# Splits on GpSimd in pieces of 512 columns, and down products of two experts in the two column halves of TensorE

## The reference

```
xl = x2 @ Wdown.T                       # x2: 1024 tokens x 256, xl: 1024 x 64
p  = top 8 of sigmoid(x2 @ Wg.T) + biases, normalised, times 2.5
for e in range(16):
    ye  = xl @ rw1[e].T * _sqrelu(xl @ rwg[e].T) @ rw2[e].T    # 64 -> 128 -> 64
    acc = acc + w_dense[:, e:e + 1] * ye
out = shared + acc @ Wup.T              # shared: the same form on x2, without a router
```

## Time and profile before

| | |
|---|---|
| median of 3 runs | 1700.2 us (1696.12 to 1702.62) |
| the profiled execution | 1699.6 us, its span 1698.3 us |
| TensorE busy | 1468.8 us, 86% |
| VectorE busy | 1240.4 us, 73% |
| ScalarE busy | 1127.9 us, 66% |
| GpSimd busy | 782.1 us, 46% |
| mean granted clock of TensorE | 0.945 |

### The profile page before, as it was taken

How to read it: one execution, slowest core, us unless ns; L and a number is a source line. 1 busy time by engine, 2 the same in 40 slices (tenths; PEclk the granted TensorE clock), 3 DMA queues, 4 the chain that set the end, 5 groups by cost and what they waited for, 6 DMA issues and landing times.

```text
span 1698.3 us, 25299 instructions
## 1 busy us (share of the span) xinstructions
PE 1468.8 (86%) x8373; PEld 713.5 (42%) x8460; DVE 1240.4 (73%) x2184; ACT 1127.9 (66%) x2020; POOL 782.1 (46%) x585
## 2 busy tenths in 40 slices
PE   5688888787878799879798989899889999999979
PEld 3243343343323243324344454444544455455445
DVE  6765766666686356568888858899689997788937
ACT  3567767658655755368677858687478776788724
POOL 3014013014020000058766848787476877577823
PEclk8697997999889999989999999999999999999989
DMA  4001200200331100010000100000000000000000
GB/s 152 1 1 33 48 2 8 53 1 5 56 114 62 51 1 5 20 39 6 1 1 20 39 20 1 6 26 1 5 25 1 26 1 1 1 1 1 1 1 26
DMA packets 20488, 36.69 MB, mean 22 GB/s; under 512 B 4898, under 2 KB 15238, under 8 KB 19334
## 3 DMA queue, kind: packets, MB, share of 16 engines
q1 hardware_dynamic: 20358, 35.07, 7.1%
HBM read 26.53 MB, written 1.15 MB: 16 GB/s over the span
## 4 chain that ended last, share of the span: by engine, by line
PE 37%; issue 7%; DVE 5%; POOL 4%; ACT 4%; POOLq 0%; ACTq 0%; DVEq 0%
PE BK L581 37%; POOL arena L1870 3%; DVE arena L1512 2%; DVE arena L1495 1%; ACT arena L1758 1%; ACT arena L1766 1%; ACT arena L1751 1%; POOL arena L1867 0%; POOL arena L1876 0%; DVE arena L886 0%; POOL arena L1847 0%; ACT L1751 0%; PE BK L866 0%; PE BK L1177 0%; POOL arena L909 0%
## 5 line engine op out<-in xcount | busy, mean ns | idle before, releaser
L581 PE MATMUL BK<-arena 128*128 128x512 bf16 (+9 forms) x8043 | 1420.8, 376 | 184.4 <-DVE arena L1495 34.0
L581 PEld LDWEIGHTS BK<-arena 128*128 128x128 bf16 (+8 forms) x8130 | 675.5, 115 | 898.4 <-issue 245.5
L1870 POOL TENSOR_TENSOR arena<-arena 128x512 f32<-128x512 f32 (+1 forms) x352 | 508.0, 1443 | 178.4 <-ACT arena L1751 154.9
L1512 DVE TENSOR_TENSOR arena<-arena 128x512 bf16<-128x512 f32 (+1 forms) x416 | 517.8, 1253 | 40.0 <-ACT arena L1758 39.6
L1751 ACT ACTIVATE arena<-BK,arena 128x512 f32<-128x512 f32 (+1 forms) x416 | 286.1, 688 | 131.2 <-PE BK L581 117.9
L1327 DVE TENSOR_REDUCE arena<-BK 128x1 f32<-128x512 f32 x384 | 244.2, 683 | 65.4 <-PE BK L581 64.1
L1659 ACT ACTIVATE arena<-BK 128x512 f32<-128x512 f32 (+1 forms) x416 | 226.1, 598 | 76.3 <-PE BK L581 69.6
L1758 ACT CAST arena<-arena 128x512 bf16<-128x512 f32 (+1 forms) x416 | 253.4, 609 | 0.0
L1766 ACT ACTIVATE arena<-BK 128x512 bf16<-128x512 f32 (+1 forms) x256 | 130.2, 508 | 88.0 <-PE BK L581 87.1
L1495 DVE CUSTOM_DVE_ANT_0 arena<-BK,arena 128x512 bf16<-128x512 f32 (+1 forms) x256 | 145.6, 569 | 37.0 <-PE BK L581 33.6
L1800 POOL TENSOR_TENSOR arena<-arena 128x256 f32<-128x256 f32 (+6 forms) x45 | 30.2, 672 | 209.3 <-ACT arena L1598 207.0
(11 more groups left out here) (170 smaller groups left out, 866.7 us busy)
## 6 DMA issues: line engine op xcount, KB each, us to landing
arena<-arena SPq DMA_DIRECT2D x144, 50.0 KB, 2.2
arena<-in_ctxT SPq DMA_DIRECT2D x8, 800.5 KB, 4.5
arena<-in_ctxk SPq DMA_DIRECT2D x4, 768.0 KB
arena<-in_wo SPq DMA_DIRECT2D x1, 2048.0 KB, 7.9
arena<-in_wqT SPq DMA_DIRECT2D x1, 2048.0 KB, 7.6
arena<-in_x SPq DMA_DIRECT2D x4, 256.0 KB, 11.0
arena<-in_rsel SPq DMA_DIRECT2D x1, 1024.0 KB, 9.2
arena<-in_rw1T SPq DMA_DIRECT2D x1, 1024.0 KB, 5.1
```

What stands on the lines that cost most here:

```text
L581: return T.matmul(out_, lhsT, rhs, start=start, stop=stop, skip_group_check=True)
L1512: V.tensor_tensor(Pl[k][0:m, :], P1[k][0:m, :], Ph[k][0:m, :], ALU.subtract).then_inc(p_low, 1)
L1870: G.tensor_tensor(acc[0:m, g % 2, :], acc[0:m, g % 2, :], P1[k][0:m, :], ALU.add).then_inc(summed1, 1)
```

## The change

Three things. GpSimd's splits are cut: the expert weights in eight pairs of a cast and a subtraction of 512 columns, `cy` in three subtractions (448, 448, 449 columns), `vc` in pieces of three tiles (384 columns). The semaphore `rw_split` counts to 8 where it counted to 1.

The down products are issued as a pair, behind every second `up`: that of the even expert into partitions 0 to 63 of bank 6, that of the odd one into 64 to 127, each half summing eight experts. `ac` copies 128 partitions, and the last product (`tl`) takes all 128 rows of `xlX` and `wu_`, which adds the halves. `dn_done` counts pairs.

For this `hh` gets a fourth buffer; the room comes from `rr`, as Relu and Square now both work in `r2`.

```diff
@@ stage1 of the plan
-                piece("dn", p)
+                if p % 2:
+                    piece("dn", p)
@@ buffers
-        rr = sb("rr", [128, 2, 512], F32, F0)
-        hh = sb("hh", [128, 3, 512], F32, F0)
+        hh = sb("hh", [128, 4, 512], F32, F0)
@@ TensorE, "dn"
-                    if p % E == 0:
+                    if p % E == 1:
                         pe.wait_ge(o_copied, 16)
                         pe.wait_ge(ac_done, p // E)
                     pe.wait_ge(*emptied("up", p, 2))
                     pe.wait_ge(ld_moe["rw2"], 16)
-                    mm(BK[6][0:64, :], rw2[:, p % E, :], hh[:, p % 3, :], start=(p % E == 0),
-                       stop=(p % E == E - 1)).then_inc(dn_done, 1)
+                    for q in (p - 1, p):
+                        hr = slice(64 * (q % 2), 64 * (q % 2) + 64)
+                        t = mm(BK[6][hr, :], rw2[:, q % E, :], hh[:, q % 4, :], start=(q % E < 2), stop=(q % E >= E - 2))
+                    t.then_inc(dn_done, 1)
@@ TensorE, "tl"
-                    mm(o, xlX[0:64, 128 * k:128 * k + 128], wu_[0:64, :], start=False).then_inc(full[i], 1)
+                    mm(o, xlX[:, 128 * k:128 * k + 128], wu_[:, :], start=False).then_inc(full[i], 1)
@@ VectorE, "up"
-                    dve.wait_ge(dn_done, s - 2)
-                    V.tensor_tensor(hh[:, s % 3, :], BK[g3][:, :], tt_[:, k, :], ALU.mult).then_inc(free[g3], 1)
+                    dve.wait_ge(dn_done, s // 2 - 1)
+                    V.tensor_tensor(hh[:, s % 4, :], BK[g3][:, :], tt_[:, k, :], ALU.mult).then_inc(free[g3], 1)
@@ ScalarE, "up" and "ac"
-                    A.activation(rr[:, k, :], BK[g2][:, :], ACT.Relu).then_inc(free[g2], 1)
+                    A.activation(r2[:, k, :], BK[g2][:, :], ACT.Relu).then_inc(free[g2], 1)
                     act.wait_ge(free[g2], n2 + 1)
-                    A.activation(r2[:, k, :], rr[:, k, :], ACT.Square).then_inc(r2_done, 1)
+                    A.activation(r2[:, k, :], r2[:, k, :], ACT.Square).then_inc(r2_done, 1)
...
-                    A.copy(xlX[0:64, :], BK[6][0:64, :]).then_inc(ac_done, 1)
+                    A.copy(xlX[:, :], BK[6][:, :]).then_inc(ac_done, 1)
@@ GpSimd, "moeld"
-                    G.tensor_copy(rwh[:, :, :], rwf[:, :, :]).then_inc(pool_chain.sem, pool_chain.up())
-                    pool.wait_ge(pool_chain.sem, pool_chain.n)
-                    G.tensor_tensor(rwl[:, :, :], rwf[:, :, :], rwh[:, :, :], ALU.subtract).then_inc(rw_split, 1)
+                    for m in range(2):
+                        for q in range(4):
+                            w_ = slice(512 * q, 512 * q + 512)
+                            G.tensor_copy(rwh[:, m, w_], rwf[:, m, w_]).then_inc(pool_chain.sem, pool_chain.up())
+                            pool.wait_ge(pool_chain.sem, pool_chain.n)
+                            G.tensor_tensor(rwl[:, m, w_], rwf[:, m, w_], rwh[:, m, w_], ALU.subtract).then_inc(rw_split, 1)
@@ GpSimd, "cy" and "vc"
-                    G.tensor_tensor(ctl[:, b, 256:S2], ctf[b][:, 0:S2 - 256], dch[b][:, :],
-                                    ALU.subtract).then_inc(ct_done, 1)
+                    for lo, hi in ((0, 448), (448, 896), (896, S2 - 256)):
+                        t = G.tensor_tensor(ctl[:, b, 256 + lo:256 + hi], ctf[b][:, lo:hi], dch[b][:, lo:hi], ALU.subtract)
+                    t.then_inc(ct_done, 1)
...
-                    G.tensor_tensor(ckl[0:m, b, lo:hi, :], ckf[0:m, lo:hi, :], ckh[0:m, b, lo:hi, :],
-                                    ALU.subtract).then_inc(ck_low, 1)
+                    for k in range(lo, hi, 3):
+                        w_ = slice(k, min(k + 3, hi))
+                        t = G.tensor_tensor(ckl[0:m, b, w_, :], ckf[0:m, w_, :], ckh[0:m, b, w_, :], ALU.subtract)
+                    t.then_inc(ck_low, 1)
```

More of the change, by code:

```diff
@@ L1129, in tensor_main @@
                         pe.wait_ge(free[i], n)
-                        pe.wait_ge(rw_split, 1)
+                        pe.wait_ge(rw_split, 8)
                         mm(BK[i][:, :], rwh[:, m, 128 * e:128 * e + 128], xl[:, ch, :], stop=False)
@@ L1451, in vector_main @@
                     dve.wait_ge(*emptied("x2", ch, 1))
-                    dve.wait_ge(rw_split, 1)
+                    dve.wait_ge(rw_split, 8)
                     V.tensor_tensor(hsh[:, ch, :], BK[i][:, :], sr[:, :], ALU.mult).then_inc(free[i], 1)
@@ L1708, in scalar_main @@
                         act.wait_ge(*emptied("up", s - 2, 0))
-                    A.activation(rr[:, k, :], BK[g2][:, :], ACT.Relu).then_inc(free[g2], 1)
+                    A.activation(r2[:, k, :], BK[g2][:, :], ACT.Relu).then_inc(free[g2], 1)
                     act.wait_ge(free[g2], n2 + 1)
-                    A.activation(r2[:, k, :], rr[:, k, :], ACT.Square).then_inc(r2_done, 1)
+                    A.activation(r2[:, k, :], r2[:, k, :], ACT.Square).then_inc(r2_done, 1)
                 elif kind == "ac":
                     ch, = arg
-                    act.wait_ge(dn_done, E * (ch + 1))
+                    act.wait_ge(dn_done, E // 2 * (ch + 1))
                     act.wait_ge(xl_done, 2)
```

## The result

The changed kernel, called after, takes 1685.9 us (median of 5 runs, 1680.8 to 1690.0) where the kernel before, called before, takes 1700.2: a ratio of 0.9919, 95% interval 0.9901 to 0.9938. The forecast was 1676. So it is faster, but 14.3 us were gained and not 24.4. The profiled execution of after took 1685.9 us, its span is 1684.5 us.

What follows compares the result with a forecast made beforehand. TensorE, 86% busy, was taken as the bound, except VectorE from 673 to 693 us and the hole at 492 to 504. Terms -8.7 + 0 - 14.7 - 1.0 = -24.4 us gave 1676 us, range 1667.5 to 1689.

Steps and rivals of the forecast that it cites:

- Part 1, the wait: At the expert-weight split, TensorE would go on at about 497.4 instead of 504.13 us: 6.7 us gained.
- Part 1, the clock: Behind the expert split, TensorE's clock would stay full through a shorter wait, gaining 2.0 of 3.3 us.
- rival (c): At the expert split, VectorE doesn't get in between pieces: +4.4 instead of -8.7 us, time 1688.9; chance 0.06.
- Part 2: GpSimd's context splits in pieces (L1847 in three, L1855 in two): 0 us, bounds -2 and +3.
- rival (e): In layer 1, cutting the context splits costs its upper bound or more: 1679 to 1684 us; chance 0.08.
- the prediction's own sign of being wrong: The stage behind the barrier before layer 1 should keep its length within 3 us; a change there refutes the prediction.
- Part 3, the price of a pair: Expert stage: two down products side by side would take 1.00 us, as one alone does.
- Part 3, how much lands on the path: Expert stage, 590 to 705 us: shorter by 14.7 us over its stretches, plus 1.0 for the last products.
- The mask's stretch: Expert stage, 673 to 693 us, bound by VectorE, which does the mask there: only 1.2 us gained.
- the last steps: End of the expert stage, 693 to 705 us: 2.4 us gained from paired down products.
- tails: Last products with 128 rows in place of 64 spare changes of tiling: 1.0 us taken of 1.6.
- rival (d): In 655 to 705 us TensorE's gaps grow and its clock falls to 1.2 GHz: up to 1721 us; chance 0.02.

Runs made afterwards that it cites:

- part 1 alone: The kernel before with only the expert-weight split cut into 16 pieces; 1691.7 us, ratio 0.9938.
- part 2: The kernel before with only the context splits (`cy`, `vc`) cut into pieces; 1699.9 us, ratio 1.0005.

## Why the prediction was right or wrong

The time lay in the range and 10 us above the forecast. Term by term:

- **Part 1, the wait (-6.7).** Right, a little low: from the start of the split TensorE goes on 7.9 us earlier. VectorE met at most one piece, as assumed.
- **Part 1, the clock (-2.0).** Wrong. From L1027 to the first Relu of stage 1 it is 85.7 us before, 87.3 in after and 87.2 in part 1 alone. The fall of the clock moved and did not go: 6.8 us at half clock begin at 493.9 us in after, and in place of one later short fall there are two, 17 us at half clock in all before and after. In eight kernels with the split in sixteen pieces the stretch from its start to stage 1 is 5.3 to 8.8 us shorter than the 97.9 of before. So part 1 gave about 7 us; rival (c) fell.
- **Part 2 (0, bounds -2 and +3).** I took the value from TensorE's waits for L1512 (19.4 us before, 19.7 after) and let GpSimd's 71% stand as room. The step that failed was to average: the 0.73 us that one `cy` takes longer is in front of one instruction (L1884) for which TensorE was just about to wait. By the traces rival (e) is what happened, 4.4 us where its bound was 3, and the prediction's own sign of being wrong, a change of the stage behind the barrier by more than 3 us, came; by the times part 2 cost less.
- **Part 3, the price of a pair (1.1 us for each of 16).** Right to 0.1 us: 1.2 us where it shows, 16.9 us less work of TensorE in stage 1, tails included.
- **Part 3, how much lands on the path.** This is the term that was mis-sized: 8.5 us for 590 to 655, where 4.5 came (from the first Relu to that of step 18, 66.0 us became 61.4); 2.6 for 655 to 673, where 0.2 came; in all -15.7 for -7.6. I had read 94% of TensorE as "bound by TensorE, so what is taken from it comes off the stage". The 94% held because the down product lay in a gap that another chain had left, and I asked only whether the pair brings a new wait of its own ("No new wait is added"). The question was what the removed product had hidden. Of the eight even steps of the first half four gained all and four next to nothing.
- **The mask's stretch (-1.2) and the last steps (-2.4, tails -1.0).** The mask's stretch gave nothing: the 20 us from 673 to 693 took 20.0 in after, VectorE's wait and the clock among them. Behind it came 2.9 us of the 3.4: 1.0 up to the last Relu, and from there to the barrier it is 23.8 us before and 21.9 in after. What of these 1.9 is the last pair's and what the tails' was not separated; with single products in alternate halves it is 22.3.
- **The clock, rival (d).** It was kept out for the reason that at 79% busy it had stayed at 1.00. With pairs it does fall; it cost about 0.9 us in after, by the estimate above, and not 45.

The ledger of the profiled pair gives -6.4 - 7.6 + 4.4 - 0.1 = -9.7 us without the chance at its head, the repeated runs -10.5 to -16.8 by the interval of the ratio. With part 1 at its usual 7 us and part 2 at the 1 to 3 us that the times show, the stages sum to -11.6 to -13.6, inside it. Why the profiled executions show more for part 2 than the times do stays open.

## What to carry to other kernels

Work that was taken off the busiest engine shortened this stage little or not at all where it had stood between two users of one buffer. Before pricing a removal, look at what is queued on the other engines at each place, and ask when the next instruction could start at the earliest. Where several small pieces share one buffer, the copy that frees it belongs ahead of the multiplications that nobody waits for soon; this order gave 7 us to the old kernel and 9 us to the new. A long instruction of GpSimd in front of a short one of VectorE is worth cutting where TensorE waits behind it, and costs where an instruction that TensorE needs stands behind it on GpSimd.

## What the runs showed of the hardware

- Two float32 products of 128x64 by 512 columns, in the two column halves, take 1.01 us together, as one alone (1.00), although each leaves two records; two of the four records start 0.01 us apart, the other two 0.48 us later.
- VectorE, blocked by GpSimd, gets in at the next border between two instructions, also where GpSimd's next one is queued: it ended 0.27 and 0.29 us behind pieces of 1.9 and 4.1 us, and the cast queued behind the second took 2.08 us in place of 1.89.
- A cast of 512 columns on GpSimd takes 0.61 us, the subtraction 1.16; the same in pieces of 2048 columns 1.89 and 4.11.
- The granted clock fell in the expert stage with every kernel that has pairs, and with none that has single products, though those had the same steps, waits of up to 1.7 us among them.
- The 14 kernels, which have the same steps up to the expert split, reach it up to 10 us apart (483.5 to 493.8 us, one execution each), while the expert stage behind it repeats to 0.1 us where its steps and the clock are the same (130.8, 130.9 and 130.9 in before, part 1 and part 2).
